# Queries and keys of a fused two-layer model as three bf16 terms instead of f32r pairs

## The reference, cut to what matters

```python
def layer0(x):                      # xn = layernorm(x)
    h = rmsnorm(xn, w); q, k, v = h @ Wq, h @ Wk, h @ Wv        # 16 heads of 8
    lin = causal_linear_attention(taylor(q @ Wqf), taylor(k @ Wkf), v)
    win = softmax(q k^T / sqrt(8), 64 rows back) @ v
    ffn = w3(gelu(h2(gelu(h1(silu(w1 xn) * (w2 xn))))))         # ternary, 128-512-512-512-128
    return x + concat(lin, win) @ Wout + ffn
def layer1(x):                      # xn = layernorm(x), affine one for the attention
    att = softmax(causal, q k^T / sqrt(8)) @ v @ Wo
    moe = sum over the top 2 of 8 experts of gate * (gelu(xn W1 + b1) W2 + b2)
    return x + att + moe
```

## Time and profile before

| | before |
|---|---|
| device time, median of 3 runs | 1272.86 us (1271.83 to 1275.03) |
| span of the profiled execution | 1269.4 us |
| PE busy | 1189.8 us, 94% |
| PE weight loads | 894.4 us, 70% |
| DVE busy | 848.0 us, 67% |
| ACT busy | 734.5 us, 58% |
| POOL busy | 665.2 us, 52% |
| DMA | 119.30 MB, mean 94 GB/s |

### The profile page before, as it was taken

The page is one execution under the profiler, slowest core; times in us unless marked ns, Lnnn a source line. Parts: engine busy times, 40 slices in busy tenths (PEclk is TensorE's granted clock), DMA queues, the critical chain, the costliest instruction groups (busy, mean ns, idle before and its releaser), DMA issues.

```text
span 1269.4 us, 26751 instructions
## 1 busy us (share of the span) xinstructions
PE 1189.8 (94%) x9122; PEld 894.4 (70%) x9122; DVE 848.0 (67%) x3390; ACT 734.5 (58%) x1561; POOL 665.2 (52%) x921
## 2 busy tenths in 40 slices
PE   5988999999999999999999999999999857989996
PEld 2566777677767776777677767776776657885896
DVE  4066597659865986588658855886588646874563
ACT  2356367736773577357745774567456524557674
POOL 4574364536443644464446444644465436675677
PEclk9999999999999999999999999999999968999999
DMA  7704420432043304230423043304330056541333
GB/s 219 210 3 162 132 77 12 158 123 92 13 160 109 106 14 159 96 120 13 158 97 119 13 151 105 117 15 137 118 117 15 11 151 147 81 66 25 45 55 39
DMA packets 88039, 119.30 MB, mean 94 GB/s; under 512 B 13736, under 2 KB 46416, under 8 KB 85904
## 3 DMA queue, kind: packets, MB, share of 16 engines
q1 hardware_dynamic: 69312, 99.66, 25.2%
q0 software_dynamic: 13792, 9.54, 5.3%
q10 hardware_dynamic: 4800, 8.39, 2.0%
HBM read 70.78 MB, written 48.46 MB: 94 GB/s over the span
## 4 chain that ended last, share of the span: by engine, by line
PE 63%; DVE 13%; ACT 10%; issue 6%; POOL 3%; DMA 3%; SPq 0%; DVEq 0%; POOLq 0%; ACTq 0%
PE bank L708 18%; PE heads L766 13%; PE bank L701 12%; PE bank L680 7%; ACT probs L1119 5%; PE bank L676 3%; PE bank L691 2%; DVE xnT_s L1579 2%; POOL out L1361 2%; PE bank L1054 2%; DVE hrow L1579 2%; DVE hT_s L1579 2%; PE bank L816 2%; PE bank L1062 1%; PE bank L685 1%
## 5 line engine op out<-in xcount | busy, mean ns | idle before, releaser
L1119 ACT ACTIVATE probs<-bank 128x512 f32<-128x512 f32 (+2 forms) x896 | 443.3, 578 | 186.5 <-PE bank L708 180.2
L1308 POOL TENSOR_SCALAR_AFFINE_SELECT probs<-probs 128x384 f32<-128x384 f32 x256 | 127.4, 520 | 211.7 <-ACT probs L1119 211.2
L708 PE MATMUL bank<-K,Q 128*128 128x192 f32 (+4 forms) x1024 | 236.5, 308 | 0.0
L708 PE MATMUL bank<-Q,K 128*128 128x192 f32 (+4 forms) x1024 | 220.7, 322 | 3.3 <-ACT probs L1119 3.1
L766 PE MATMUL heads<-probs,V 128*18 128x192 f32 (+9 forms) x3072 | 196.1, 396 | 6.6 <-POOL probs L1311 3.9
L708 PEld LDWEIGHTS bank<-K,Q 128*128 128x128 f32 x1024 | 166.5, 189 | 21.7 <-issue 9.6
L708 PEld LDWEIGHTS bank<-Q,K 128*128 128x128 f32 x1024 | 152.3, 194 | 39.5 <-issue 17.5
L766 PEld LDWEIGHTS heads<-probs,V 128*9 128x9 f32 (+1 forms) x3072 | 78.5, 94 | 114.0 <-issue 75.6
L1361 POOL DMA_INDIRECT out<-h1T_s x78 | 123.1, 1578 | 60.0 <-ACT h1T_s L1269 35.6
L708 PE MATMUL bank<-QM,K 128*128 128x512 f32 (+3 forms) x512 | 138.4, 336 | 4.6 <-ACT probs L1119 3.8
L1261 ACT ACTIVATE h2T_s<-bank,h1T_s 128x128 f32<-128x128 f32 x312 | 89.2, 368 | 91.8 <-PE bank L1054 88.9
(11 more groups left out here) (224 smaller groups left out, 2184.9 us busy)
## 6 DMA issues: line engine op xcount, KB each, us to landing
Q<-slots_of_q SPq DMA_DIRECT2D x15, 1024.0 KB, 8.0
K<-low_of_h SPq DMA_DIRECT2D x13, 1024.0 KB, 7.8
QM<-slots_of_qm SPq DMA_DIRECT2D x8, 1024.0 KB, 6.0
K<-slots_of_k SPq DMA_DIRECT2D x60, 128.0 KB, 2.7
K<-slots_of_k SPq DMA_DIRECT2D x68, 96.0 KB
slots_of_q<-Q SPq DMA_DIRECT2D x24, 256.0 KB, 3.0
slots_of_k<-QM SPq DMA_DIRECT2D x24, 256.0 KB, 4.0
slots_of_qm<-Q SPq DMA_DIRECT2D x24, 256.0 KB, 4.2
```

The lines of the kernel that those rows point to most:

```text
L708: mm = pe.matmul(to[:, at:at + right.shape[1]], left, right, start=True, stop=True, skip_group_check=True)
L1119: return act.activation(to, bank, func, scale=scale, bias=bias).then_inc(taken_sem(run, unit), 1)
L1308: pool.affine_select(out=three, in_=three, compare_op=ALU.is_ge, fill=0.0, base=0, pattern=[[0, 3], [1, P]], channel_multiplier=-1)
```

## The change

Queries and keys become three bf16 terms (high, mid, low, each what the terms before left over), in 64 rows a head: eight slots of 8 rows, of which six hold products of terms (high with high, mid and low; mid with high and mid; low with high), one the maximum in two bf16 parts and one constants. A group has two heads instead of four, so the contraction still has 128 rows, and the number of score matmuls and their columns stay. `Q1`, `QM`, `Q2` become [128, 8, 512] bf16, of the same size in bytes; `K1` and `K2b` keep their shape in bf16 and half the bytes. The bytes sent and fetched for a name stay, in rows of 1 KB instead of 2 KB; keys are fetched whole in two DMAs a half instead of four, constants and all.

- ACT makes the high term as before. DVE makes the f32 rest from the bank (and waits for its own operation before it raises a semaphore). The mid term, a cast of the rest, is made by POOL for q1, k1 and qm1, behind its slide masks, and by ACT for k2 and q2 and in the opening. The low term, rest minus mid, is made by POOL for the former and by DVE for the latter.
- In `dense_stage` DVE now runs rest of k2, rest of q2, low of k2, low of q2, and then `take xnT2`, which the logits need. ACT runs high k2, high q2, mid k2, DMA of q2's high term, mid q2, DMA of the mid term, gelu of h2_2, DMA of the low term. Each DMA writes all slots of its term.
- `negate_max` is two DVE operations, the second waiting for the first; `place_max` still has four DMAs.
- The low halves get buffers of their own, over which the experts' weights `W1` and `W2` lie. Saves and loads of low halves, the waits of PE on them, `set_keys` and the restoring of zeros in each batch are gone. `load_experts` is issued at the head of SP's last body, when the last hidden layers are done, instead of after the last slide unit.
- SP stores the result before it loads x, and sends the mid and low terms of q1, k1 and qm1 after that.

```diff
-        Q2 = sb("Q2", [P, G, T], F32R)
+        Q2, K2b, K1 = sb("Q2", [P, SG, T], BF16), sb("K2", [P, H, T], BF16), sb("K1", [P, H, T], BF16)
         with ExitStack() as aside:
-            K2b = sb("K2", [P, H, T], F32R, aside)
-        whole_b = sb("whole_b", [P, H, T])[:, H // 2:H // 2 + FC, :]
+            low_a, low_h1, low_b, low_h2 = (sb(n, [P, FC, T], F32R, aside) for n in ("low_a", "low_h1", "low_b", "low_h2"))
+        W1, W2 = sb("W1_s", [P, E, T]), sb("W2_s", [P, E, FC, P])
+        whole_a, whole_b = W1[:, 0:FC, :], W2[:, 0:FC, :, :].rearrange("p e c n -> p e (c n)")
...
+            def send(sequence, name, n):
+                sem = ("high", "mid", "low")[n]
+                sp.wait_ge(S[f"{sem}_{name}"], due(f"{sem}_{name}", sequence, 1))
+                sp.dma_start(slots_view(name, n), slots_src(name, n)).then_inc(S[f"sent_{name}"], 16)
...
                 if after:
                     for name in ("q1", "k1", "qm1"):
-                        split_and_send(run, (b, 1), name)
...
+                        send((b, 1), name, 0)
                 if before and this:
                     store(run, b - 1)
+                if this and after:
+                    load_x((b, 1), (b + 2) & (NB - 1))
+                if after:
+                    for n in (1, 2):
+                        for name in ("q1", "k1", "qm1"):
+                            send((b, 1), name, n)
...
+            def split_mid(sequence, name):
+                act.wait_ge(S[f"rest_{name}"], due(f"rest_{name}", sequence, 1))
+                act.activation(parts_of[name][1], rest_of[name], ACT.Identity).then_inc(S[f"mid_{name}"], 1)
...
-                    split_hi(run, now, "k2", bk1[:, 0:1])
-                    split_hi(run, now, "q2", bq1[:, 0:1])
-
-                    view = scratch["q2"].rearrange("h (s d) t -> s h d t", d=D)
-                    high, low = parts_of["q2"]
-                    act.wait_ge(S["hi_q2"], due("hi_q2", now, 1))
-                    for s in (0, 1):
-                        act.dma_start(view[s], high.bitcast(F32)).then_inc(S["sent_q2"], 16)
+                    split_high(run, now, "k2", bk1[:, 0:1])
+                    split_high(run, now, "q2", bq1[:, 0:1])
+                    split_mid(now, "k2")
+                    act.wait_ge(S["high_q2"], due("high_q2", now, 1))
+                    act.dma_start(slots_view("q2", 0), slots_src("q2", 0)).then_inc(S["sent_q2"], 16)
+                    split_mid(now, "q2")
+                    act.wait_ge(S["mid_q2"], due("mid_q2", now, 1))
+                    act.dma_start(slots_view("q2", 1), slots_src("q2", 1)).then_inc(S["sent_q2"], 16)
                     if after:
                         gelu(run, "h2_2", hidden_c[2], sh2[:, 2:3])
...
+            def split_rest(sequence, names):
+                for name in names:
+                    pool.wait_ge(S[f"rest_{name}"], due(f"rest_{name}", sequence, 1))
+                    pool.tensor_copy(parts_of[name][1], rest_of[name]).then_inc(S[f"mid_{name}"], 1)
+                for name in names:
+                    pool.wait_ge(S[f"mid_{name}"], due(f"mid_{name}", sequence, 1))
+                    pool.tensor_tensor(parts_of[name][2], rest_of[name], parts_of[name][1], ALU.subtract).then_inc(S[f"low_{name}"], 1)
...
                 if after:
-                    pool.wait_ge(full_sem(run, "h1_3"), full_at(run, "h1_3"))
-                    clear(K1, HALVES["k1"]).then_inc(S["keys1_restored"], 1)
+                    split_rest(nxt, ("q1", "k1", "qm1"))
...
                 dve.wait_ge(full_sem(run, unit), full_at(run, unit))
-                dve.tensor_scalar(mrow[:, :], bank_of(run, unit)[0:mrow.shape[0], 0:P], -1.0, None, ALU.mult).then_inc(taken_sem(run, unit), 1)
+                top = bank_of(run, unit)[0:mrow.shape[0], 0:P]
+                dve.tensor_scalar(mrow[:, 0, :], top, -1.0, None, ALU.mult).then_inc(S[sem], 1)
+                dve.wait_ge(S[sem], due(sem, sequence, nth))
+                dve.scalar_tensor_tensor(out=mrow[:, 1, :], in0=top, scalar=-1.0, in1=mrow[:, 0, :], op0=ALU.mult, op1=ALU.subtract)\
+                    .then_inc(taken_sem(run, unit), 1)
...
-                    split_lo(run, now, "k2", bk1[:, 0:1])
-                    split_lo(run, now, "q2", bq1[:, 0:1])
+                    split_rest(run, now, "k2", bk1[:, 0:1])
+                    split_rest(run, now, "q2", bq1[:, 0:1])
+                    split_low(now, "k2")
+                    split_low(now, "q2")
                     if not after:
                         run_tiles(MIXED, QUERIED)
                     take(run, "xnT2", xnT[:, :])
```

More of the change, by code:

```diff
@@ L22 @@
 ROWS = 32
+SG, SH = H // 2, 2
+SROWS = 64
+SLOT = 8
+AT_MAX = 6
+SLOTS_Q, SLOTS_K = ((0, 3, 1), (3, 5, 1), (5, 6, 1)), ((1, 6, 2), (0, 5, 4), (2, 3, 1))
+ONE_PAIR = 1.0 + 0x3F80 / 2 ** 23
 FC = 4
@@ L491, in send @@
[L491 to L494, removed]
-            LOWER, UPPER = slice(0, G // 2), slice(G // 2, G)
-            def fetch(name, groups=slice(0, G), sem="slots", restored=False):
+            def send(sequence, name, n):
+                sem = ("high", "mid", "low")[n]
+                sp.wait_ge(S[f"{sem}_{name}"], due(f"{sem}_{name}", sequence, 1))
+                sp.dma_start(slots_view(name, n), slots_src(name, n)).then_inc(S[f"sent_{name}"], 16)
@@ L499, in fetch @@
+            LOWER, UPPER = slice(0, SG // 2), slice(SG // 2, SG)
+            def fetch(name, groups=slice(0, SG), sem="slots"):
                 to = slots_to[name]
                 if name in ("k1", "k2"):
-                    by_row, rows = scratch[name].rearrange("(g i) r t -> i r g t", i=HG), 4 * D if restored else 3 * D
-                    for i in range(HG):
-                        sp.dma_start(to[ROWS * i:ROWS * i + rows, HG * groups.start + i:HG * groups.stop:HG, :].bitcast(F32), by_row[i][0:rows, groups])\
+                    by_row = scratch[name].rearrange("(g i) r t -> i r g t", i=SH)
+                    for i in range(SH):
+                        sp.dma_start(to[SROWS * i:SROWS * (i + 1), SH * groups.start + i:SH * groups.stop:SH, :], by_row[i][:, groups])\
@@ L550, in body @@
                 part, b = run
+                if not after:
+                    load_experts()
                 if before and this:
@@ L1192, in slide_stage @@
                     if n == 8 and after:
-                        split_hi(run, nxt, "q1")
-                        split_hi(run, nxt, "k1")
+                        split_high(run, nxt, "q1")
+                        split_high(run, nxt, "k1")
                     if n == 10 and after:
-                        split_hi(run, nxt, "qm1")
+                        split_high(run, nxt, "qm1")
+                        if not this:
+                            for name in ("q1", "k1", "qm1"):
+                                split_mid(nxt, name)
                     if n == GATES_AT and after:
@@ L1824, in beside_scores @@
                     if a == PAIRS + turned_at(before):
-                        negate_max(run, "slide_max", mrow_s)
+                        negate_max(run, "slide_max", mrow_s, "negated_s", now, 1)
                         if after:
@@ L1868, in slide_stage @@
                     if n == 12 and after:
-                        split_lo(run, nxt, "qm1")
+                        split_rest(run, nxt, "qm1")
+                        if not this:
+                            for name in ("q1", "k1", "qm1"):
+                                split_low(nxt, name)
                     if n == 15 and before:
```

225 lines of the change are left out of this document (100 added, 125 removed), and 4 rows, old and new, of the table counts.

## The result

The changed kernel takes 1292.17 us (median of 4 runs, 1290.89 to 1296.23) against 1272.66 us for the kernel before in the same session: a ratio of 1.0154, 95% interval 1.0135 to 1.0174. The profiled execution's span is 1289.1 us against 1269.4, 19.7 us longer.

What follows compares the result with a forecast made beforehand. DVE, not the 94% busy PE, was taken to bound the causal maxima. Removed 13.6 us against added 21.7 and 9.8 for the clock gave net +17.9, a forecast of 1291 us, range 1258 to 1301.

Steps and rivals of the forecast that it cites:

- The bound: Stretch of causal row maxima: DVE busy 16.73 of 16.90 us, so a faster PE only waits longer there.
- the ceiling: Score matmuls on PE: most that faster bf16 operands could save, 6.9 us a batch, 55 in all, if PE limited everywhere.
- (a): bf16 operands in L708, refills of the ring after `weigh` groups: 1.1 us a batch less, 8.8 in all.
- (b): bf16 operands in the slide stage: 0.5 us a batch less, 4 us in all.
- (c): Earlier load of the experts' weights, for which DVE had idled 1.87 us: 0.8 us less.
- (e): Chain to the logits, `take xnT2` behind the low terms of k2 and q2: 2.1 us a batch more, 16.8 in all.
- (f): `negate_max` as two dependent DVE operations: 0.35 us each, 0.7 us a batch more in 7 batches, 4.9 in all.
- (g): POOL's mid and low terms of q1, k1, qm1 after the slide masks, 7.7 us in idle time: costs nothing.
- (h): Half-size keys in fewer and shorter packets, loads at the batch's head: nothing, bounds -1 to +1 us a batch.
- The clock: Longer PE wait before the logits brings falls to half clock: 1.4 us in seven batches, 9.8 us more.
- Rival B: Whole kernel: slower, but without the clock's fall, 1281 us; chance 0.25.
- Rival C: Whole kernel: faster because PE is the limit, 1239 us at full price, 1266 at half; chance 0.20.

Runs made afterwards that it cites:

- experiment 4: Kernel before, with all score and maximum matmuls reading the upper 16 bits of their f32r operands as bf16 by a stride of two; 1256.28 us, ratio 0.9877.
- experiment 5: Changed kernel with the second operation of each negation left out, the low part of the maximum a zero; 1286.84 us, ratio 1.0113.
- experiment 1: Changed kernel with four filling matmuls of 512 columns in PE's wait before the logits, in seven batches; 1281.20 us, ratio 1.0064.
- experiment 2: Changed kernel with two filling matmuls of 512 columns in PE's wait before the logits, in seven batches; 1279.63 us, ratio 1.0051.
- experiment 3: Kernel before, f32r operands kept, with two extra DVE copies ahead of the take of xnT2 in seven batches; 1285.69 us, ratio 1.0089.
- second kernel of experiment 9: Changed kernel with xnT2 taken ahead of q2's rest, gelu of h2_2 ahead of the mid terms, one operation a negation; 1272.35 us, ratio 0.9995.
- experiment 10: The second kernel of experiment 9 with k2's low term made by POOL instead of DVE in seven batches; 1273.00 us, ratio 0.9992.

## Why the prediction was right

The forecast was 1291, the measured time 1292.17. The two losses that it names are there, the longer way to the logits and the clock, but the total is closer than its terms, and that closeness is luck. By the steps of the prediction:

- **The bound (causal maxima on DVE).** Right. Loads faster by 92 ns each gave 1.8 us a batch against the ceiling of 6.9. Part of what was gained is read from DVE's gaps behind `weigh`, as predicted: 1.18 us where the earlier trace rows had 1.40. The loads take half their time (98 instead of 189 ns), not a third as the prediction had it from the earlier trace rows.
- **(a), (b): 1.6 us a batch, 12.8 in all.** Experiment 4: 16.3 us, 1.8 a batch and most of the rest in the last batch, whose period fell from 125.8 to 122.3. The estimate was a fifth too low.
- **(c): 0.8 us.** In the traces 1 us, in the times nothing that can be seen.
- **(e): 2.1 us a batch.** Measured: 2.41-0.83 = 1.6. The copies and subtractions were right (0.63 and 0.69 us), the path was not. The prediction led it over ACT, whose mid of q2 should have started late behind a DMA issue of 0.73 us, with DVE's low of q2 waiting for it. The issue takes 0.37 us and delays nothing: mid q2 waits for DVE's rest, and DVE's second subtraction starts right behind the first. The path stays on DVE: two subtractions, and two waits of 0.15 us for its own result, which the sum had left out.

```profile
680.12 0.63 ACT L1110 ACTIVATE Q<-xs 128x512 bf16<-128x512 f32 x1
680.13 0.37 ACTq L1242 DMA_DIRECT2D slots_of_q<-Q  x1
681.03 0.63 ACT L1110 ACTIVATE Q<-Q 128x512 bf16<-128x512 f32 x1 [0.27 <-DVEq L1556]
```

- **(f): 0.7 us a batch, 4.9.** The operation itself is as reckoned: in DVE's timeline it starts 0.31 us behind the first and takes 0.28. What it costs is not: the 5.3 us of experiment 5 look like a match, but without the falls it is 0.2 to 0.3 us a batch, some 2 in all. Its lines in the changed kernel:

```profile
586.89 0.27 DVE L1615 TENSOR_SCALAR mrow_c<-bank 32x128 bf16<-32x128 f32 x1
587.20 0.28 DVE L1617 SCALAR_TENSOR_TENSOR mrow_c<-bank,mrow_c 32x128 bf16<-32x128 f32 x1
```

- **(g), (h): nothing.** POOL's six operations run from 654.4 to 660.4 and no wait of PE ends on them or on a fetch of theirs. One premise of (h) was wrong: the packets did not become fewer, the whole kernel has 123,961 where it had 88,039, and a fetch of 1 MB of queries lands in 10.9 instead of 8.0 us (medians). In the changed kernel that stayed hidden.
- **The clock: 1.4 us in seven batches, 9.8.** That a longer wait brings falls was right (experiments 1, 2 and 3), and the size was off. One slice costs 1.6 us (8.77 from logits to third layer, against 7.19 in the batch of experiment 5 that has none), where 1.4 was taken, but four of seven batches have two slices, and two more falls came elsewhere. Experiment 2, with no fall behind the logits and three elsewhere, puts the whole at 1292.2-1279.6+4.1 = 17 us; the traces, batch by batch, put it at 17.5 behind the logits and 3 for the other two, 20 us.

So without the clock the changes would come to between -1 and +3 us, where the sum had +8.1: the gain was 3.5 us too small, the chain 4 us and the negations 3 us too large; against them stands the way to the first logits, 2.2 us longer, which had no term (a part of it is the clock's, which also fell for 3.4 us more there). The clock's term was 7 to 10 us too small. These errors offset each other. Rival B (no falls) would have been 1272 to 1276 rather than 1281. Rival C (PE as the limit) is refuted by experiment 4: 0.3 of the ceiling of 55 us was delivered, where C needed more than 0.4. On the page "Perfetto Trace Analysis" of the Trainium skill, section "Identifying the Most-Contended Engine", the prediction had weighed 70% of weight-load busy time: halving the score matmuls' share of those loads (experiment 4) moved the time by 1.2%. The trace speaks against reading the share over the whole span: in the causal stretch, where these loads are, DVE was full before and after.

What stays open is the exact condition for a fall. 0.69 and 0.83 us before the logits never brought one, nor did the one wait of 1.05 us in experiment 2; 1.20 us and more did in 33 of the 35 batches of the five kernels that have it there. But 1.35 us before the maxima did in only four of seven batches (second kernel of experiment 9) and in three of seven (experiment 10), and the two waits of 0.59 us at the end of the slide stage, which are in every steady batch of the changed kernel, were followed by a fall in two of six batches there (386.7 and 912.4) and in three in experiment 2. No run tells these batches from the others.

## What to carry to other kernels

Before pricing a faster operand for the busiest engine, read stage by stage who empties its results; where that one is full, the gain is only what it starves by. Price every wait of PE twice, by its length and by the clock that it may cost: here 1.6 us more of wait cost another 2.4 us a batch by the half clock behind it, and 1.8 us of useless matmuls inside the wait gave most of the latter back. When a variant seems to match its forecast, compare the falls of the two traces first: 3.5 of the 5 us that one operation seemed to cost were theirs. And moving one operation ahead rarely ends such a wait: look for the next one hidden behind it (a bank, then a consumer) and add up the work of the engine in the middle before building.

## What the runs showed of the hardware that I had not expected

- One wait of PE brought one or two slices of 3.4 us at 1.2 GHz, differing from batch to batch of one execution, so that kernels with such waits scatter (1279 to 1292 us in experiment 3, at mean clocks of 0.982 down to 0.972) where the kernel before stays within 1270 to 1278 in all sessions.
- A bf16 operand read with a stride of two elements (experiment 4) cost nothing that can be seen: 97 ns a load against 98 contiguous in the changed kernel, and 248 ns for a 192-column matmul in both.
- One DMA from ACT's queue, 384 KB from one source to three slots, was issued in 0.37 us, where two of 256 KB to a slot each had taken 1.46.
- A 512-column matmul with f32 operands that aren't f32r (the fillers of experiments 1 and 2) is two records that start 0.43 us apart.
